# A transformer block on one core: the joining maximum and the transposition one unit later in the loop of maxima, and another order in the tail

## What is computed

```python
x = x + 0.5 * ffn(layernorm(x))
x = x + attention(layernorm(x))       # 16 heads of 8, rotary q and k, softmax over 2048 keys
x = x + 0.5 * ffn(layernorm(x))

def ffn(x):                            # 128 -> 512 -> 128
    h = gelu(x @ absmean(W_fc).T)
    return layernorm(h, ln_w, ln_b) @ absmean(W_proj).T
```

## Time and profile before

| | before |
|---|---|
| median of the runs | 769.03 us (3 runs, 769.03 to 938.7) |
| profiled execution, whole | 770.04 us |
| its span, first to last instruction | 767.9 us |
| mean granted TensorE clock | 0.961 |
| busy: PE, DVE, ACT, POOL | 727.3, 692.5, 637.5, 257.4 us |
| DMA | 12.45 MB, mean 16 GB/s |

### The profile page before, as it was taken

One profiled execution on the slowest core, in us unless ns is written; L12 is line 12 of the kernel. 1 busy time (PEld: TensorE's weight loads), 2 busy tenths in 40 slices (PEclk: granted clock), 3 DMA queues, 4 the chain that ended last, 5 costly groups with the idle time before them and its releaser, 6 DMA issues.

```text
span 767.9 us, 17532 instructions
## 1 busy us (share of the span) xinstructions
PE 727.3 (95%) x6843; PEld 249.4 (32%) x6843; DVE 692.5 (90%) x880; ACT 637.5 (83%) x1196; POOL 257.4 (34%) x526
## 2 busy tenths in 40 slices
PE   6899779999999999999999999999999999999994
PEld 2774211222222222222222222222222222224473
DVE  5778659999999999999999999999999999996382
ACT  3443653899999999999999999999999999999742
POOL 4332001455445455233332222232222232425221
PEclk9999955999999999999999999999999999999997
DMA  7000000000011011011000000000000000000000
GB/s 219 2 1 0 1 1 1 3 4 5 24 25 25 24 25 25 25 24 40 4 4 5 4 4 4 6 17 5 4 4 4 5 7 20 8 6 4 5 29 28
DMA packets 22674, 12.45 MB, mean 16 GB/s; under 512 B 13088, under 2 KB 21152, under 8 KB 22336
## 3 DMA queue, kind: packets, MB, share of 16 engines
q1 hardware_dynamic: 11328, 8.77, 4.1%
q0 software_dynamic: 9056, 2.04, 1.6%
q10 hardware_dynamic: 2208, 0.53, 0.4%
HBM read 7.34 MB, written 2.33 MB: 13 GB/s over the span
## 4 chain that ended last, share of the span: by engine, by line
DVE 65%; PE 25%; issue 4%; ACT 3%; DMA 1%; DVEq 0%; POOL 0%; POOLq 0%; SPq 0%; ACTq 0%
DVE mh L818 59%; PE ps L1337 7%; PE ps L1324 5%; PE ps L1305 3%; PE ps L1124 2%; PE ps L1224 2%; PE ps L1183 2%; PE ps L1200 1%; DVE ring L680 1%; ACT KT L1029 1%; DVE top L826 1%; PE ps L1354 1%; DMA X<-in_L_attn_x_dram 1%; PE ps L1210 0%; DVE rope L843 0%
## 5 line engine op out<-in xcount | busy, mean ns | idle before, releaser
L818 DVE TENSOR_REDUCE mh<-ps 128x2 f32<-128x1024 f32 x512 | 584.9, 1218 | 7.0 <-PE ps L1305 6.9
L1080 ACT ACTIVATE ring<-ps 128x512 f32<-128x512 f32 x1024 | 551.5, 600 | 34.4 <-PE ps L1324 16.2
L1337 PE MATMUL ps<-ring,Vx 128*32 128x256 f32 x4096 | 325.6, 392 | 0.9 <-ACT outT L1088 0.9
L1305 PE MATMUL ps<-KT,QT 48*128 48x512 bf16 x1024 | 209.8, 393 | 10.6 <-DVE mh L818 10.4
L1324 PE MATMUL ps<-QT,KT 51*128 51x512 bf16 x1024 | 212.8, 389 | 1.1
L1337 PEld LDWEIGHTS ps<-ring,Vx 128*32 128x32 f32 x4096 | 82.1, 108 | 157.6 <-ACT ring L1080 142.1
L1324 PEld LDWEIGHTS ps<-QT,KT 51*128 51x128 bf16 x1024 | 51.8, 93 | 219.7 <-ACT ring L1080 205.2
L548 POOL DMA_DIRECT2D rope<-outT x80 | 43.1, 544 | 180.0 <-ACT outT L1088 171.1
L537 POOL DMA_DIRECT2D QT<-mrow x128 | 72.0, 568 | 42.0 <-DVE mrow L835 38.5
L1305 PEld LDWEIGHTS ps<-KT,QT 48*128 48x128 bf16 x1024 | 50.0, 94 | 67.1 <-DVE mh L818 30.2
L525 POOL TENSOR_TENSOR mp<-zeros,top 128x8 bf16<-128x8 f32 x32 | 6.4, 200 | 193.2 <-DVE top L826 193.2
(11 more groups left out here) (133 smaller groups left out, 351.8 us busy)
## 6 DMA issues: line engine op xcount, KB each, us to landing
rope<-rope_tables SPq DMA_DIRECT2D x2, 1024.0 KB, 6.1
QT<-mrow SPq DMA_DIRECT2D x128, 0.8 KB
QT<-mrow POOLq DMA_DIRECT2D x128, 0.8 KB, 1.7
rope<-outT SPq DMA_DIRECT2D x80, 8.0 KB
rope<-outT POOLq DMA_DIRECT2D x80, 8.0 KB, 1.7
q_bounce<-XB SPq DMA_DIRECT2D x3, 384.0 KB, 2.4
QT<-q_bounce SPq DMA_DIRECT2D x18, 64.0 KB
QT<-q_bounce POOLq DMA_DIRECT2D x18, 64.0 KB, 3.3
```

Of the source, the lines that this page charges most:

```text
L818: v.tensor_reduce(mh[:, n // A_STEP % 2, :, q, kb], ps[:, bank:bank + 2, :], AX.X, ALU.max)\
L1080: a.activation(ring[:, n % PRING, :], ps[:, exp_bank(n), :], ACT.Exp, scale=SCALE).then_inc(p_ready, 1)
L1305: mm = t.matmul(ps[:, A0 + 2 * (n % 2) + h, :], QT[rows, j, at:at + P], KT[rows, j, kb * CS:(kb + 1) * CS], start=True, stop=True)
L1337: mm = t.matmul(ps[r:r + 32, PO, 0:QH], Vx[:, kt, col:col + 32], ring[:, (2 * n + h) % PRING, half * QH:(half + 1) * QH], start=(kt == 0), ...
```

## The change

In the loop of maxima `whole_max(g)` moves from behind unit 15 of its group to behind unit 0 of the next (`TOP_AT`), and `max_rows(g)` from behind unit 1 of the next group to behind unit 2 (`CUT_AT`). The last group's stays right behind the last unit.

In the tail, block 0 of the expansion of step 4 becomes a late item ("H") at tile 27 of the last group; two of the last four value tiles go ahead of block 1. The last output projection gets bank 7 (`TP`) and no longer waits for a gelu. On TensorE it stands ahead of the sums of squares of step 4, and the last transposition ahead of those of step 5; the expansion of step 6 is in its plain order. On VectorE the reciprocals and the product come ahead of the squares of step 4, the addition of the last chunk ahead of the variance, its normalization ahead of the update, `take` ahead of the variance of step 5, and the squares of step 7 ahead of the update of step 6. On GpSimd the last `ln_scale` goes ahead of the first `hidden_scale`.

```diff
-CUT_AT = 2
+TOP_AT = 1
+CUT_AT = 3
...
-        (NG - 1, 11): ("F", 0), (NG - 1, 15): ("F", 1), (NG - 1, 23): ("F", 2)}
+        (NG - 1, 11): ("F", 0), (NG - 1, 15): ("F", 1), (NG - 1, 23): ("F", 2), (NG - 1, 27): ("H", 0)}
...
-            return late_tiles(A0 + c % 2 if c < NC - 1 else FC)
+            return late_tiles(A0 + c % 2 if c < NC - 1 else TP)
...
             sums(NG - 1)
+            ln_scale(2, NC - 1, NC - 1)
             hidden_scale(1, 0)
-            ln_scale(2, NC - 1, NC - 1)
...
-                if u == A_STEP - 1:
-                    whole_max(g)
+                if g and u == TOP_AT - 1:
+                    whole_max(g - 1)
                 if g and u == CUT_AT - 1:
                     max_rows(g - 1)
...
+            whole_max(NG - 1)
             max_rows(NG - 1)
...
-            add_squares(NC)
             reciprocals(NC - 1)
             dve.wait_ge(od_rec, NC)
             v.tensor_tensor(OT[:, (NC - 1) * CS:NC * CS], OD[:, (NC - 1) % 2, 0, :], OD[:, (NC - 1) % 2, 1, :],
                             ALU.mult).then_inc(ot_ready, 1)
+            add_squares(NC)
+            output_chunk(NC - 1)
             variance(NC)
-            output_chunk(NC - 1)
+            norm_rows(2, X2, NC - 1, NC - 1)
             update(NC)
-            norm_rows(2, X2, NC - 1, NC - 1)
             add_squares(NC + 1)
+            take(NC - 1)
             variance(NC + 1)
-            take(NC - 1)
             update(NC + 1)
             add_squares(NC + 2)
             variance(NC + 2)
+            add_squares(NC + 3)
             update(NC + 2)
-            add_squares(NC + 3)
             variance(NC + 3)
             update(NC + 3)
...
-                    else:
-                        pe.wait_ge(h_ready, (c - 2 + NC) * KH + 1)
...
+                elif kind == "H":
+                    pe.wait_ge(taken, 2)
+                    expand_block(NC, 0)
...
+            pv_tile(NG * NT - 4)
+            pv_tile(NG * NT - 3)
             pe.wait_ge(taken, NC - 1)
-            expand_block(NC, 0)
             expand_block(NC, 1)
-            for n in range(NG * NT - PV_LAG - 2, NG * NT):
-                pv_tile(n)
+            pv_tile(NG * NT - 2)
+            pv_tile(NG * NT - 1)
...
             contract(NC)
+            late("O", NC - 1)
             sum_squares(NC)
-            late("O", NC - 1)
-            for k in range(1, KH):
-                expand_block(NC + 2, k)
+            expand(NC + 2)
             pe.wait_ge(x2_ready, NC)
-            expand_block(NC + 2, 0)
             contract(NC + 1)
+            late("F", NC - 1)
             sum_squares(NC + 1)
-            late("F", NC - 1)
             contract(NC + 2)
```

## The result

The changed kernel takes 763.89 us in the median (5 runs, 763.32 to 766.44), the kernel before 769.63 beside it: a ratio of 0.9937 with a 95% interval of 0.9912 to 0.9962 (one slow run of the kernel before, 938.7 us, is left out of the ratio). The profiled execution took 763.32, with a span of 761.4 in place of 767.9: 6.5 less, against 5.9 in the sum. In another comparison the same kernel took 766.05 against 770.0 (0.9937 again, 0.9918 to 0.9957).

What follows compares the result with a forecast made beforehand. VectorE's row maxima bound the loop, followed by a tail; 3.9 + 0 + 0.6 - 0.5 + 1.9 = 5.9 us off the profiled 770.04 gives 764.1, median 763.1. Range 762 to 764.5 (chance 0.62).

Steps and rivals of the forecast that it cites:

- the sum: Whole kernel: the saved times of loop and tail added together, 5.9 us less than before.
- the wide range: Whole kernel: run time between 760.5 and 767.3 us, leaving out the slower case and some of the edges.
- The loop: Loop of maxima: moved joining maximum no longer waits for its direct predecessor, 0.13 saved at 30 group boundaries, 3.9 us.
- One unit more is covered. Cost: 0.: Loop of maxima: rows reach GpSimd and the DMA queues 1.13 us later, hidden by the loop's lead, cost 0.
- TensorE becomes the bound: Rival, loop: TensorE's 18.2 a group is 0.1 too low, half the loop's gain goes, 765.0 us; chance 0.08.
- The expansion block: Last group: moving the first expansion block ahead reorders TensorE's work, removes none; 0 us, bound 0.3 either way.
- The middle of the tail: Tail, steps 4 to 6: reciprocal and product first gain 0.6 us; last transposition waiting for a gelu loses 0.5.
- The end: End of tail: squares ahead of the update let TensorE's last sums start right behind the last contraction, 1.9 us saved.
- something better: Rival, whole kernel: an unplanned gain such as a clock rising earlier after the slow slices; no size, chance 0.05.
- The wait was free: Rival, loop: removing the own-engine wait brings nothing, only the tail gains, 767.0 us; chance 0.10.
- The clock drops in the tail: Rival, tail: clock falls briefly behind TensorE's light stretch of 2.9 us, 1.6 lost, 764.7 us; chance 0.10.
- Not given back: Rival, tail: clock falls and stays down, 12 us more of TensorE work, 775 us, slower than before; chance 0.05.

Runs made afterwards that it cites:

- the longer stretch: Changed kernel with the last transposition waiting for the fourth gelu of step 6 instead of the second: 767.67 us against 770.03 for the kernel before, ratio 0.9972.

## Why the prediction was right, point by point

The time and the direction held: 763.89 against 763.1. How close it came is in part luck. In the other comparison the median was 766.05, outside the 762 to 764.5 that got the largest chance and inside the wide range. The ratio, the same both times, is 4.8 us, where 5.9 was forecast. The terms together were 0.7 us too high, and in the profiled execution an earlier rise of the clock, 1.3 us, hides that.

*The loop.* Mechanism right and now shown from both sides (18.28 without the wait, 21.29 with one at each maximum). The size was 3.9; in the table it came out as 3.25. The count of 30 boundaries was right: one of them lies just ahead of the table's point, and its 0.22 stands in the row above, so that the loop gave 3.47 = 3.9 - 0.45. The step that failed is the sentence "One unit more is covered. Cost: 0." It took a typical landing for the landing in every group. Where both queues issued larger DMAs right behind the rows, these needed 2 us more: 6.24 from the transposition, with a cover of 5.7. Before the change the cover was one maximum longer, and no score matmul waited for rows. The rival "TensorE becomes the bound" didn't come: by the waits VectorE stood for TensorE 9 times for 6.2 us in all, before 9 times for 6.9, and inside the loop only in the group of the late rows. But it was close: in the loop (145 to 688) TensorE's weight loads of L1305 waited for a maximum 32 times before, 8.0 us in all (the earlier trace rows shows one), and 3 times for 1.6 now. By this the two engines are about even, and a further gain on VectorE alone should bring little; that wasn't tried.

*The expansion block.* That it "reorders this work and removes none" was right. "Cost and gain 0; bound: 0.3 either way" was wrong: 0.43 lost, outside the bound. A group of matmuls broken in two costs 0.1 to 0.2 more in this mix, and the take-out came later by the whole of it.

*The middle of the tail.* 0.6 gained and 0.5 lost were forecast; 0.63 and 0.46 came (0.38 of it between the two contractions, 0.08 in the expansion ahead of them). The reciprocal started 4.27 behind the take-out (722.22), by the estimate 4.2.

*The end.* 1.9 forecast, 1.92 measured, and the same 2.0 when taken back alone.

*What was not in the sum.* The sum of terms that the change really has is 3.47 - 0.43 + 0.63 - 0.46 + 1.92 + 0.1 = 5.2, not 5.9. The profiled pair differs by 6.5, and the 1.3 on top goes with the clock, which rose 2.7 us earlier at the start of the loop: 2.7 us at full instead of half clock are 1.35 us of TensorE's work. The "something better" of the chances was this, but as scatter between executions and not as a result of the change. The ratio of the runs, 0.9937, is 4.8 us, with an interval from 2.9 to 6.8: it fits the corrected sum, and can't tell it from the forecast. That the runs give a little less than the stretches, here and for the tail alone (1.1 against 1.8), would fit the falls of the clock in some executions; that isn't shown.

*The rivals.* "The wait was free" fell. "The clock drops in the tail" came true in two traces of the changed kernel's relatives, at the forecast price; in neither of the two profiles of the changed kernel itself. "Not given back" was seen in none: in the two traces the clock was up again behind 742.6 and 742.8, and with the longer stretch behind 746.8.

## What to carry to other kernels

On VectorE, an instruction that waits for its direct predecessor gave up the overlap of the two, here 0.13 to 0.19 us each time: put one independent instruction between them, and look in the timeline for a start to start that is longer than its neighbours'. When that delays something else by a unit, check its cover in the group with the worst company on the DMA queues, not in a typical one. In a tail that several engines share, the largest gain was the cheapest to see: an engine waiting for work that was ready, but queued behind an update which itself waited for a third engine.

## What the runs showed of the hardware

- The own-engine wait on VectorE costs 0.13 us for a small reduction in SBUF behind a 1.22 us reduction from PSUM, and 0.19 for one such reduction behind another.
- SyncE's four small DMAs of rows landed 3.69 us after the last of them began to be issued (the median for GpSimd's, from issue to landing, is 1.7) when three of 64 KB with small packets were issued on each of two queues within 0.2 and 0.8 us behind it. Where one of the two queues came 2.2 us or more later, no matmul waited for the rows.
- One fp32 expansion block by itself holds TensorE for 1.06 us, two together for 1.91.
- GpSimd's closing DRAIN took 8.32 us in twelve of the traces and 8.98 in the two of kernels in which it issues six groups of DMAs at another place; the span ended 0.2 us behind it.
- The moment at which the clock rises again scatters between executions of one kernel; the third group of the changed kernel began at 138.65 in one profile and 142.70 in another.
